# Attention and mixture of experts in one kernel: experts paired from the third on, a third PSUM bank, late inputs and reordered chains

## The reference

```
k = layernorm(x);  v = ctx
# per channel, over the 128 tokens of a batch (WKV recurrence)
y_t = (e^(pp-q) * aa + e^(u+k_t-q) * v_t) / (e^(pp-q) * bb + e^(u+k_t-q));  aa, bb decay by e^(-e^time_decay)
x = x + y
h = rmsnorm(layernorm(x)) * norm_w
scores = softmax(h @ gate_w.T)              # 32 experts, the 4 best of each token, weights normed to 1
routed = sum over the 4 of weight * ((silu(h @ w13_g[e]) * (h @ w13_u[e])) @ w2[e])   # capacity 256 rows an expert
shared = (silu(h @ shared_gate) * (h @ shared_up)) @ shared_down
out = x + layernorm(x) + routed + shared
```

## Time and profile before

| | |
|---|---|
| median of three runs | 163.81 us |
| the profiled execution | 165.11 us, span 163.3 us |
| PE busy | 135.1 us (83%) |
| DVE busy | 114.1 us (70%) |
| ACT busy | 91.4 us (56%) |
| POOL busy | 85.5 us (52%) |
| indirect DMAs on POOL | 32 of about 1.0 us into rows_in, 49 of about 1.0 us into rows_out |
| loads of an expert's rows (L273), 264 KB each | 32, median 4.7 us from issue to landing |
| HBM read and written | 27.95 MB and 20.48 MB |

### The profile page before, as it was taken

The page is one execution under the profiler, slowest core; times in us unless marked ns, Lnnn a source line. Parts: engine busy times, 40 slices in busy tenths (PEclk is TensorE's granted clock), DMA queues, the critical chain, the costliest instruction groups (busy, mean ns, idle before and its releaser), DMA issues.

```text
span 163.3 us, 2856 instructions
## 1 busy us (share of the span) xinstructions
PE 135.1 (83%) x740; PEld 114.9 (70%) x740; DVE 114.1 (70%) x415; ACT 91.4 (56%) x262; POOL 85.5 (52%) x106
## 2 busy tenths in 40 slices
PE   0254598889886799597979999998999999999591
PEld 0233397879775787285869988987999989888350
DVE  0489989999998633516997788787766787734471
ACT  3623777877777624025847798887845776210011
POOL 8200004777777774720557767777664677671000
PEclk9999999999999999969999999999999999999999
DMA  4999999999999981679989999997766321285977
GB/s 103 288 379 420 420 417 412 385 382 370 375 382 373 373 293 72 151 218 291 365 250 332 381 351 377 366 342 237 209 197 166 118 87 64 69 308 180 354 270 257
DMA packets 32433, 46.49 MB, mean 285 GB/s; under 512 B 3017, under 2 KB 27285, under 8 KB 32156
## 3 DMA queue, kind: packets, MB, share of 16 engines
q1 hardware_dynamic: 27936, 37.15, 67.3%
q0 software_dynamic: 3888, 8.53, 14.4%
q10 hardware_dynamic: 588, 0.54, 1.0%
HBM read 27.95 MB, written 20.48 MB: 297 GB/s over the span
## 4 chain that ended last, share of the span: by engine, by line
PE 53%; DVE 15%; DMA 12%; ACT 9%; issue 6%; POOL 1%; ACTq 1%; SPq 0%; DVEq 0%; POOLq 0%
PE bank L1055 20%; PE bank L1072 11%; PE bank L1041 6%; DMA w_all<-rows_out 5%; DVE S L639 4%; DVE ND L652 2%; PE bank L940 2%; DMA rows_out<-w_all,pick_idx 2%; PE bank L977 2%; PE bank L964 2%; PE bank L955 2%; PE bank L950 2%; DMA xg<-rows_in 2%; ACT n_row L507 2%; ACT ln_den L484 2%
## 5 line engine op out<-in xcount | busy, mean ns | idle before, releaser
L384 POOL DMA_INDIRECT rows_out<-w_all,pick_idx x49 | 48.2, 985 | 28.9 <-DVE w_all L873 10.0
L370 POOL DMA_INDIRECT rows_in<-n_row,slot_all x32 | 32.7, 1023 | 32.3 <-DVE slot_all L733 21.5
L1055 PE MATMUL bank<-xT,w_all 128*128 128x128 f32 (+2 forms) x256 | 41.3, 305 | 1.5 <-issue 1.2
L1055 PEld LDWEIGHTS bank<-xT,w_all 128*128 128x128 f32 x256 | 36.1, 193 | 4.1 <-issue 3.7
L539 ACT ACTIVATE xT<-bank,nws 128x256 f32<-128x256 f32 x64 | 26.9, 471 | 14.9 <-PE bank L1041 14.6
L1072 PE MATMUL bank<-w_all,act_t 128*128 128x256 f32 x92 | 25.3, 382 | 1.0 <-DVE act_t L867 1.0
L867 DVE TENSOR_TENSOR act_t<-sg,bank 128x256 f32<-128x256 f32 x32 | 13.4, 419 | 13.7 <-ACT sg L544 13.6
L544 ACT ACTIVATE sg<-bank 128x256 f32<-128x256 f32 x32 | 12.3, 383 | 9.5 <-PE bank L1055 8.7
L1072 PEld LDWEIGHTS bank<-w_all,act_t 128*128 128x128 f32 x92 | 15.6, 191 | 2.5 <-issue 1.7
L1041 PE MATMUL bank<-ident,xg 128*128 128x128 f32 x92 | 15.8, 280 | 1.5 <-DMA xg<-rows_in 1.4
L1041 PEld LDWEIGHTS bank<-ident,xg 128*128 128x128 f32 x92 | 12.1, 143 | 5.4 <-issue 2.5
(11 more groups left out here) (143 smaller groups left out, 228.7 us busy)
## 6 DMA issues: line engine op xcount, KB each, us to landing
w_all<-in_L_ffn_w_dram SPq DMA_DIRECT2D x12, 1024.0 KB, 14.3
rows_in<-w_all SPq DMA_DIRECT2D x8, 1056.0 KB, 16.1
xg<-rows_in SPq DMA_DIRECT2D x32, 264.0 KB, 4.7
w_all<-rows_out SPq DMA_DIRECT2D x2, 1024.0 KB, 5.4
w_all<-rows_out SPq DMA_DIRECT2D x2, 512.0 KB, 7.1
w_all<-rows_out SPq DMA_DIRECT2D x4, 256.0 KB, 8.0
rows_out<-w_all,pick_idx POOLq DMA_INDIRECT x49, 2.9
x_all<-in_x_dram SPq DMA_DIRECT2D x1, 768.0 KB, 6.1
```

Source lines behind the costliest of these rows:

```text
L370: pool.indirect_dma_start(rows_in, bass.IndirectOffsetOnAxis(ap=slot_all[:, b, k:k + 1], axis=0), n_row[:, b, :], None)\
L384: pool.indirect_dma_start(rows_out, bass.IndirectOffsetOnAxis(ap=pick_idx[:, e, a:a + 1], axis=0), yo[e][:, a, :], None, bounds_check=PICK ...
L1055: last = nc.tensor.matmul(FG[j][:, a, lo:lo + slots], w13_all[:, expert(e), h, a, :], xT[:, j, h, lo:lo + slots], start=(h == 0), stop=(h ...
```

## The change

- Singles are i = 0 and i = 1 (four scatters), then 15 pairs (2, 3) to (30, 31). Of a pair's second expert DVE copies the main half and adds the extra half apart. G[0] and G[1] now wait for scatters 1 to 46 (i up to 29), G[2] and G[3] for 47 to 49 (i = 30, 31).
- x and v of batches 6 and 7 are a third piece (`THIRD`), issued on SP behind the eight stores of zeros. DVE takes their moments in step 4, and `others_shift` of step 4 waits for the scales from ACT, which stand in `exp_k(6)`, the last stage of ACT's step 4.
- ACT makes e^k of batch 0 ahead of the small constants; DVE and PE wait for those later.
- YT rotates over three banks (2, 3, 5), NT has bank 4 alone; `residual_in` of batch n + 1 stands behind `positions` in step n; the last batch's `to_tokens` stands ahead of `normed_to_channels`.
- The logits wait for each half of hT by itself; of the eight parts of the shared expert one stands ahead of the last logits, one ahead of TOT, six behind it. One of the two `shared_down(1)` matmuls is moved ahead of the first rows.
- PE does transposes and gate/up of both experts 0 and 1 before the transposes of expert 2.
- Where an expert has over 128 and not over 192 rows, the second half's two transposes take 64 rows instead of 128, in a nested branch.

```diff
+THIRD = 6
-EARLY_OUT = 2 + 3 * (PAIRS - 1)
+EARLY_OUT = 4 + 3 * (PAIRS - 1)
-        YT = [bank[2 + j][:, 0:C] for j in range(2)]
-        NT = [bank[4 + j][:, 0:C].rearrange("p (h t) -> p h t", h=HC) for j in range(2)]
+        YT = [bank[q][:, 0:C] for q in (2, 3, 5)]
+        NT = bank[4][:, 0:C].rearrange("p (h t) -> p h t", h=HC)
...
         def first_of(m):
-            return 2 * m + 1
+            return 2 * m + 2
...
+            sp.dma_start(x_all[:, THIRD:B, :], xv[:, THIRD:B, :]).then_inc(s["x2_in"], 16)
+            sp.dma_start(v_all[:, THIRD:B, :], vv[:, THIRD:B, :]).then_inc(s["v2_in"], 16)
             sp.dma_start(sgu[:, :, 0, :], sh_gate.rearrange("(h p) f -> p h f", p=P)).then_inc(s["sh_in"], 16)
...
-                if r == 1:
+                if r == K - 2:
                     sp.wait_ge(row_out[1], 48)
-                if r == K - 1:
-                    sp.wait_ge(row_out[2], 32)
...
             single_out(0, 1, 1, row_out[0])
+            single_out(1, 2, 2, row_out[0])
...
-            single_out(E - 1, PAIRS + 2, ALL_YO, row_out[2])
...
             first_scales(0, 0, FIRST)
+            first_exp()
...
                 if b == FIRST:
-                    first_scales(1, FIRST, B)
+                    first_scales(1, FIRST, THIRD)
+                if b == THIRD:
+                    first_scales(2, THIRD, B)
...
             def others_stats(b, j):
                 if b == 0:
                     dve.wait_ge(s["x1_in"], 16)
-                    first_stats(FIRST, B)
+                    first_stats(FIRST, THIRD)
+                if b == THIRD - 2:
+                    dve.wait_ge(s["x2_in"], 16)
+                    first_stats(THIRD, B)
 
             def others_shift(b, j):
                 if b == 0:
-                    first_shift(1, FIRST, B)
+                    first_shift(1, FIRST, THIRD)
+                if b == THIRD - 2:
+                    first_shift(2, THIRD, B)
...
                 if b == B - 1:
                     pe.wait_ge(s["base_ready"], B - 1)
                     pe.wait_ge(s["sh_in"], 32)
-                    for h in range(HC):
-                        shared_part(0, 0, h)
-                pe.wait_ge(s["hT_ready"], HC * (b + 1))
+                    shared_part(0, 0, 0)
...
-            run([(0, residual_in), (2, slots_so_far), (-1, to_channels), (2, positions), (1, normed_to_channels), (0, to_tokens), (1, logits)])
+            run([(2, slots_so_far), (-1, to_channels), (2, positions), (-1, residual_in), (0, last_to_tokens),
+                 (1, normed_to_channels), (0, to_tokens), (1, logits)])
...
+                more = extra(expert(e))
+                first_rows = (0, MORE - P) if more else (2 * P - MORE, P)
                 with pe.If(second != 0):
-                    transpose_half(e, j, extra(expert(e)))
-                transpose_half(e, j, main(expert(e))).then_inc(s["f_xt"], 1)
+                    with pe.If(third != 0):
+                        transpose_rows(e, j, more, 0, P)
+                    with pe.Else():
+                        transpose_rows(e, j, more, *first_rows)
+                transpose_rows(e, j, main(expert(e)), 0, P).then_inc(s["f_xt"], 1)
...
-            rows_to_channels(0, 0, second(0))
-            shared_down(1)
-            for e in range(E + 1):
-                if e == 0:
-                    gate_up(0, 0, second(0), third(0))
+            rows_to_channels(0, 0, second(0), third(0))
+            shared_down(1, 1)
+            rows_to_channels(1, 1, second(1), third(1))
+            gate_up(0, 0, second(0), third(0))
+            gate_up(1, 1, second(1), third(1))
+            for e in range(1, E + 1):
                 if e + 1 < E:
-                    rows_to_channels(e + 1, (e + 1) % 2, second(e + 1))
+                    rows_to_channels(e + 1, (e + 1) % 2, second(e + 1), third(e + 1))
...
```

## The result

The changed kernel takes 168.83 us (167.87 to 169.72, 4 runs), the kernel before 163.72 (163.08 to 164.35, 4 runs): ratio 1.0311, 95% interval 1.0238 to 1.0384. It is 5.1 us slower; 161.6 was forecast. The profiled execution took 167.87, span 166.1, against 165.11 and 163.3. Medians in this text are of all runs and ratios of those in the faster of two states only, so a kernel with slow runs can show a median above what its ratio gives (e5: 164.39 us, ratio 0.9966).

What follows compares the result with a forecast made beforehand. It took DVE to bound the loop, PE the experts and latencies the seams; -2.0 us (first experts, with the end of attention) + 0 (narrow transposes) + 0 (tail) - 0.2 (later loads) made -2.2: median 161.6 us, range 159.6 to 163.9.

Steps and rivals of the forecast that it cites:

- Another -0.2: Experts: earlier row numbers shorten later loads, about -0.2 us, added in the final sum.
- Start and loop: Attention up to the last scan: start -1.45, loop -1.1, step 4 +0.85 and +1.7 us, together 0.0.
- wait for positions: Loop: DVE no longer waits for positions once residual_in stands behind them; four waits, -1.1 us.
- the late input: Step 4: x and v of the last batches arrive in time; no wait taken, bounds 0 and 2 us.
- the wait in step 4: DVE's others_shift waits for ACT's scales, so that step's scan starts +1.7 us later; bounds 0.8 to 2.2.
- End of attention and first experts: Row numbers 1.05 us sooner, transposes of expert 3 at 75.0 to 75.6: -2.0 us, bounds -0.8 and -3.0.
- rival (a): First experts: PE's clock stays at its upper level and narrow transposes pay; 159.8 us, chance 0.15.
- Narrow transposes: Experts: 64-row transposes of 13 experts change nothing, 0 us; bounds +0.6 (nested branch) and -1.4.
- persists since PE stays the limit: Experts: the first experts' gain of 2.0 us lasts to the end, as PE remains the limit.
- Tail: Last scatters, gathers and sums: regrouped waits change nothing, 0 us; bounds -1.0 and +1.8.
- the prediction's own sign of being wrong: Tail: the forecast is wrong if the last gather's start stands idle behind scatter 49.
- rival (b): Tail: last scatters land only when 2 MB of gathers are through, +1.9 us; 163.5, no change; chance 0.15.

Runs made afterwards that it cites:

- e5: e7 with the changed kernel's expert groups and gather waits (so the changed kernel with 128-row transposes and early scales): 164.39 us, ratio 0.9966.
- e7: e6 with ACT's scales of batches 6 and 7 moved ahead, behind first_reciprocal of step 4: 161.53 us, ratio 0.984 to the kernel before.
- g2: e7 with the 64-row transposes and their nested branch back, in a clean session: 165.03 us, ratio 1.003 to the kernel before.
- e10: e5 with G[0] and G[1] also asked only behind scatters 47 to 49, in a disturbed session: 185.05 us, ratio 1.0153.
- e6: The changed kernel with 128-row transposes and the expert groups and gather waits of the kernel before: 163.44 us, ratio 0.9955.
- a2: The changed kernel measured again beside the kernel before, in another clean session: 169.61 us, ratio 1.031 (1.026 to 1.0361).

## Why the prediction was wrong

Differences between the profiled executions, changed less before. The prediction works out its tail without the 2.0 us of the first experts; they are taken off here, as in its last paragraph (G[0] asked near 142.5, last gather landed near 157.2). Another -0.2 stands in its sum alone.

```
step                                  forecast   measured
scan of batch 1                         -1.45      -1.90
last scan (start and loop)               0.0       -0.9
last row numbers                        -1.05      -1.8
transposes of expert 3                  -2.0       -2.3
lead left at the last down              -2.0       -0.25
scatter 49 handed over                  -2.4       -1.1
G[0] asked                              +0.6       +1.9
from there to the last gather landed    -2.6       +0.4
from there to the end                    0.0       +0.5
span                                    -2.2       +2.8
```

- **Start and loop: right, a little small.** No wait for positions is left, the late input costs 0.26 us (0.3 to 1.2 in the other clean profiles) where none was forecast, and the wait in step 4 is there: 1.87 us, where 1.7 was worked out. e7 shows that it need not be paid.
- **End of attention and first experts: the number right, in part by luck.** 74.96 stands against the forecast 75.0 to 75.6. The shared parts took 3.8 us for six and not 5.2, so PE was through early and waited for the first rows, 1.76 and 0.70 us: the load set the first transposes, at 67.60, where PE was to set them at 68.9. What this gained went into the two gate/ups, 3.69 us instead of 2.2, since the granted clock fell to 0.50 at 70 us as it had before; so rival (a) fell by its own condition.
- **Narrow transposes: the first step that failed.** It was taken at 0 with an upper bound of +0.6, by the rows of two loop matmuls, and measured +2.0 in the trace and 3.1 us by the ratio of g2. Those rows hold operands of 128 rows on both sides; they say nothing of a change of height between neighbours. The Trainium skill (TensorE: Matmul & The Clock Gate, LDWEIGHTS) has a load of fewer rows take the same time, and the trace agrees (137 and 142 ns); the idle time of 0.24 us before such a load is what the prediction left out. The bound of +0.6 was put on the branch, which costs nothing. Why the loads start late no profile here shows, nor whether the half rows or the half columns do it.
- **The gain that "persists since PE stays the limit": wrong for that reason.** PE stayed the limit, and its own work grew by the 2.0.
- **Tail: the second, and the larger in the trace.** It was taken at 0, bounds -1.0 and +1.8; from the last down to the end it is +3.0. The later ask for G[0] was in the forecast (+2.6 against the old ask). What was to pay for it was the reading back: scatter 49 lands 3.9 us after its handover, so the latency of the last 2 MB hides behind the first two, and the 4 MB take 14.3 to 14.9 us instead of 17.3. This is the step that failed. Scatter 49 landed after 7.06 us, at 152.6, when the 2 MB were through, and the reading back took 17.7; the last gathers stood behind scatter 49, as the prediction's own sign of being wrong has it. That is rival (b), which priced the tail 1.9 us longer; it had chance 0.15. The last 0.5 us come behind the last landing: the granted clock is 0.50 from 158 to 161, behind the 4 us in which PE had 1.26 us of work, and PE's last sums end later. The Trainium skill (DMA: Bandwidth & Descriptors, Queues, rings and completion order) has each engine take turns between queues; no run here bears out that this brings a scatter through early: it landed later by 2.0 us with the first megabyte and 2.7 with the second, against 3.0 for reading one.
- **What forecast and rivals missed:** the reading back takes 16.8 to 17.7 us from the ask for G[0], whether G[0] alone or G[0] and G[1] stand beside the last scatters. So there a later ask is paid in full; e10, with none beside them, pays its 4 us for the most part back. The new groups hand the last scatters over sooner, which gains nothing by itself, and leave three of them instead of five behind the one that G[0] waits for.

Do the parts close? By ratios of clean sessions: e7 0.984; late scales times 1.012 (e6 over e7); groups times 1.013 (e5 over e7); narrow times 1.019 (g2 over e7): 1.028, inside a2's 1.026 to 1.036 (each of these ratios is known to about 0.4%). In us from 163.7: -2.6 + 1.9 + 2.1 + 3.1 = +4.5 of the measured 5.1. The narrow transposes and the groups cost 5.2 us against the 0.7 that the rest of the change gains (e6). Open is why g2 lies 3.1 us over e7 by the ratios when its trace accounts for 2.4 to 2.6; 0.5 us is within what two such ratios can be off.

## What to carry to other kernels

A cheaper-looking operand shape has to be priced by rows in which it stands between the neighbours that it will have; a pair of rows of one shape each doesn't bound it. At a tail of writes and dependent reads, price the reading back from the moment at which the first read can be asked: a regrouping that hands over the last write sooner and asks for the first read later can lose. Latency hides behind reads under way only if the write that gates the next ones gets through beside them, and here it didn't. And where a bound is argued for one mechanism (here the branch), it is no bound for the step.

## What the hardware showed beyond that

A second half's two 64-row transposes with the main half's two stand, between 128-row matmuls, 0.53 us behind the start of the down and 0.54 us ahead of the next gate/up; with 128-row ones it is 0.43 and 0.44. A handed-over scatter lands after 2.19 us alone, 3.4 to 4.3 beside 1 MB of gathers, 5.9 to 7.2 beside 2 MB. With one or two gathers beside the last scatters, 4 MB were read back in 16.8 to 17.7 us; with none, in 13.5.
